# A warped-image transformer block on one core: 16 groups of 4 x 8 pixels, gathers in two bursts an image, one strips load moved

## The reference, cut to what matters

```python
x = x + rigid(x, dx, angle)   # each pixel: bilinear sample of its own image at a rotated, shifted place
x = x + ffn(x)                # relu(x wi^T + 2 x a^T b^T + expert lora) -> the same with wo; F = 2048
x = x + pooled(x)             # tanh scores, masked softmax over rows, p @ x / count
x = x + adapter(x)            # per-language 512 -> 128 -> 512, residual, layer norm, gamma, beta

# in rigid(X, dx, angle):
xp = c * gx - s * gy + dx[:, 0]
yp = s * gx + c * gy + dx[:, 1]
ix = (yp / h * 2.0 + 1.0) * 0.5 * (w - 1)
iy = (xp / w * 2.0 + 1.0) * 0.5 * (h - 1)
out = the four neighbours of (iy, ix), weighted by distance, 0 outside the image
```

## Time and profile before

| | |
|---|---|
| three runs | 2302.42, 2303.27, 2307.72 us (median 2303.27) |
| the profiled execution | 2311.27 us, span from first to last instruction 2309.6 |
| PE, DVE, ACT, POOL busy | 2098.2, 1964.2, 874.6, 947.5 us |
| granted TensorE clock, mean | 0.958 of full speed |
| gathers (L584) | 512, 1.32 us each on POOL |
| products (L853) | 4,096, 0.284 us each on DVE |

### The profile page before, as it was taken

The page is one execution under the profiler, slowest core; times in us unless marked ns, Lnnn a source line. Parts: engine busy times, 40 slices in busy tenths (PEclk is TensorE's granted clock), DMA queues, the critical chain, the costliest instruction groups (busy, mean ns, idle before and its releaser), DMA issues.

```text
span 2309.6 us, 53794 instructions
## 1 busy us (share of the span) xinstructions
PE 2098.2 (91%) x15230; PEld 1453.4 (63%) x15230; DVE 1964.2 (85%) x6594; ACT 874.6 (38%) x2292; POOL 947.5 (41%) x1066
## 2 busy tenths in 40 slices
PE   7678999989989998999999899999999989999996
PEld 3336667666666676666666666666666666667673
DVE  7578899989888898889989898898888898899943
ACT  2323444433433443343334343333433333344431
POOL 3434444454453444434434443453344344444201
PEclk9659999999999999999999999999999999999997
DMA  8683555665555556545655664465566455554322
GB/s 220 151 214 85 129 142 131 143 150 128 134 115 133 129 130 151 129 129 117 148 126 129 141 151 123 110 143 131 128 132 149 118 116 138 128 136 114 98 72 64
DMA packets 336489, 303.57 MB, mean 131 GB/s; under 512 B 187294, under 2 KB 255976, under 8 KB 335766
## 3 DMA queue, kind: packets, MB, share of 16 engines
q1 hardware_dynamic: 290358, 184.05, 33.1%
q0 software_dynamic: 42624, 109.35, 20.2%
q10 hardware_dynamic: 3168, 6.29, 0.9%
HBM read 273.73 MB, written 65.70 MB: 147 GB/s over the span
## 4 chain that ended last, share of the span: by engine, by line
DVE 46%; PE 28%; issue 15%; DVEq 5%; SPq 2%; DMA 1%; another core or an unknown queue 1%; ACT 1%; POOL 0%; ACTq 0%; POOLq 0%
DVE work L853 17%; PE bank L1343 9%; PE bank L1381 8%; DVE work L866 4%; DVE work L867 4%; DVE work L865 4%; DVEq L849 2%; DVEq L838 2%; DVE work L809 2%; PE bank L1199 2%; DVE warp_sum L880 2%; DVE hidden_parts L913 2%; PE bank L1375 1%; DVE warp_sum L876 1%; PE bank L1275 1%
## 5 line engine op out<-in xcount | busy, mean ns | idle before, releaser
L1343 PE MATMUL bank<-x1T,wiT 128*128 128x256 f16 x6144 | 765.3, 275 | 15.6 <-issue 14.8
L1381 PE MATMUL bank<-woT,hidden_parts 128*128 128x512 f16 x3072 | 755.9, 383 | 0.0
L853 DVE TENSOR_TENSOR work<-work 128x72 f32<-128x72 f32 x4096 | 683.5, 284 | 70.5 <-issue 48.2
L584 POOL DMA_INDIRECT work<-strips,gather_now x512 | 675.9, 1320 | 158.9 <-issue 136.6
L1343 PEld LDWEIGHTS bank<-x1T,wiT 128*128 128x128 f16 x6144 | 602.6, 99 | 163.7 <-issue 67.3
L1167 ACT ACTIVATE hidden<-bank 128x256 f32<-128x256 f32 x512 | 196.7, 384 | 767.0 <-PE bank L1350 446.8
L1381 PEld LDWEIGHTS bank<-woT,hidden_parts 128*128 128x128 f16 x3072 | 281.9, 99 | 247.2 <-issue 9.8
L580 POOL TENSOR_TENSOR gather_now<-group_now,no_offset 128x8 int32<-128x8 int32 x64 | 30.5, 476 | 792.9 <-DVE work L853 792.4
L913 DVE TENSOR_TENSOR hidden_parts<-hidden,hidden_parts 128x512 f16<-128x512 f32 x256 | 176.9, 691 | 29.2 <-ACT hidden_parts L1169 13.5
L1375 PE MATMUL bank<-hidden_parts,experts 128*128 128x128 f16 x2048 | 200.7, 221 | 0.0
L1169 ACT ACTIVATE hidden_parts<-bank 128x256 f16<-128x256 f32 x512 | 195.1, 381 | 0.0
(11 more groups left out here) (191 smaller groups left out, 2402.9 us busy)
## 6 DMA issues: line engine op xcount, KB each, us to landing
strips<-in_x_dram SPq DMA_DIRECT2D x64, 532.0 KB
lw<-in_L_cond_W_dram SPq DMA_DIRECT2D x128, 256.0 KB
xs<-in_x_dram SPq DMA_DIRECT2D x64, 256.0 KB
experts<-ib_dram SPq DMA_DIRECT2D x64, 256.0 KB
gamma_b<-in_L_cond_gamma_dram SPq DMA_DIRECT2D x64, 256.0 KB
x<-in_L_cond_beta_dram POOLq DMA_DIRECT2D x64, 256.0 KB, 5.9
out_dram<-y SPq DMA_DIRECT2D x64, 256.0 KB, 2.5
work<-strips,gather_now POOLq DMA_INDIRECT x512
```

The lines of the kernel that those rows point to most:

```text
L584: g.indirect_dma_start(out=win[:, k, gi, :], out_offset=None, in_=flat, in_offset=bass.IndirectOffsetOnAxis(at, 0)).then_inc(gathered[k], 16)
L853: last = v.tensor_tensor(prods[:, :, :, j, :, row].rearrange("p a b g -> p g b a"), seen, wx.unsqueeze(2).broadcast_to([128, NG, TAPS, TAP ...
L1343: t.matmul(b[:, 0:2 * T], wiT[:, ws, m, tile(f)], x1T[:, xs_, m, :], start=(m == 0 and ws + xs_ == 0), stop=False)
L1381: last = t.matmul(down_ps[k][:, :], hidden_parts[:, hs, f % RING, k * T:(k + 1) * T], woT[:, ws, f, :], start=(first and n == 0), stop=False)
```

## The change

- A group is 4 columns by 8 rows (`GC`, `GR`), and a partition holds 16 groups instead of 8. `Q` is 32 instead of 64, so an image takes 32 product instructions of 144 elements, 16 gathers of 226 elements, and 8 offsets a register load.
- The strips have 64 columns instead of 76, and an image takes three strip transfers instead of five.
- `gather` sends only the groups `first` to `end`. Each image's 16 gathers go in two bursts of eight. Image 0's second burst waits for `hidden_low(4)` of the pair, image 1's second burst for `hidden_low(0)` of the next pair and stands behind `add_beta` there.
- SP loads image 0's strips at the beginning of the pair instead of behind `load_lang`.
- The Newton iteration moves from POOL to DVE (`deviations`, 12 instructions with the guess, just ahead of `finish`); POOL does none of it.
- DVE's loop has four bodies a turn instead of two (`Fori(1, NP // 4 - 1)`).
- The address tables ahead of the loop have 1,024 columns instead of 512 and lie in `work`. `beta_b` is gone; its staging use goes to `x1T`.

```diff
-GP = 8
-NG = 8
-Q = GP * GP
+GC, GR = 4, 8
+NG = 16
+Q = GC * GR
 HALF = Q // 2
-LOADED = 32
...
-SW, SS = 76, 32
-LEFT = 2 * SS
+SW, SS = 64, 32
+LEFT = SS
...
-RUN = 4 * SW + 44
+RUN = 3 * SW + 34
...
-                src = bass.AP(img.tensor, img.offset, [[SS, NS - 5], [D, T], [1, SW]])
-                sp.dma_start(strips[s, 2:NS - 3, rows, :], src).then_inc(strips_in[s], 16)
-                for n in range(2):
-                    before = LEFT - n * SS
-                    sp.dma_start(strips[s, n, rows, before:SW], img[:, 0:SW - before]).then_inc(strips_in[s], 16)
-                    left = LEFT - n * SS
-                    sp.dma_start(strips[s, NS - 3 + n, rows, 0:left], img[:, D - left:D]).then_inc(strips_in[s], 16)
+                src = bass.AP(img.tensor, img.offset, [[SS, NS - 3], [D, T], [1, SW]])
+                sp.dma_start(strips[s, 1:NS - 2, rows, :], src).then_inc(strips_in[s], 16)
+                sp.dma_start(strips[s, 0, rows, LEFT:SW], img[:, 0:SW - LEFT]).then_inc(strips_in[s], 16)
+                sp.dma_start(strips[s, NS - 2, rows, 0:SS], img[:, D - SS:D]).then_inc(strips_in[s], 16)
...
             def body(i, q):
+                if there(i, -3):
+                    load_strips(i + 3, 0, 1 - q)
                 if there(i, 0):
                     load_expert_oa(i)
...
-            def gather(a, k, par):
+            def gather(a, k, par, first=0, end=NG, lows=None):
 
                 n, s = a * 2 + k, 2 * par + k
                 pool.sem_clear(pool_chain)
-                pool.wait_ge(pix_in[s], (a - par) * 24 + 48)
-                pool.wait_ge(strips_in[s], (a - par) * 40 + 80)
-                ge(pool, win_used, n - 1)
+                if not first:
+                    pool.wait_ge(pix_in[s], (a - par) * 24 + 48)
+                    pool.wait_ge(strips_in[s], (a - par) * 24 + 48)
+                    ge(pool, win_used, n - 1)
+                if lows is not None:
+                    pool.wait_ge(hidden_ready, lows)
...
             def body(i, q):
                 if there(i, 2):
                     add_beta(i - 2, q)
-                    deviations(i - 2)
-                for k in range(2):
-                    if there(i, -2):
-                        gather(i + 2, k, q)
+                if there(i, -1) and there(i, 0):
+                    gather(i + 1, 1, 1 - q, NG // 2, NG, i * (FT // 2) + 1)
+                if there(i, -2):
+                    gather(i + 2, 0, q, 0, NG // 2)
+                    gather(i + 2, 0, q, NG // 2, NG, i * (FT // 2) + 5 if there(i, 0) else None)
+                    gather(i + 2, 1, q, 0, NG // 2)
...
-                def guess_deviations():
+                def deviations():
 
                     link(v.tensor_scalar(var_eps[:, :], mv[:, :, 1], EPS, None, ALU.add))
                     link(v.tensor_scalar(guess_i[:, :], var_eps[:, :].bitcast(i32), 1, None, ALU.arith_shift_right))
-                    v.tensor_scalar(rstd[:, :].bitcast(i32), guess_i[:, :], -1.0, float(0x5F3759DF), ALU.mult, ALU.add).then_inc(guess_ready, 1)
+                    link(v.tensor_scalar(rstd[:, :].bitcast(i32), guess_i[:, :], -1.0, float(0x5F3759DF), ALU.mult, ALU.add))
+                    for step in range(3):
+                        link(v.tensor_tensor(newton[:, :], rstd[:, :], rstd[:, :], ALU.mult))
+                        link(v.scalar_tensor_tensor(newton[:, :], newton[:, :], -0.5, var_eps[:, :], ALU.mult, ALU.mult))
+                        link(v.scalar_tensor_tensor(rstd[:, :], newton[:, :], 1.5, rstd[:, :], ALU.add, ALU.mult))
...
-            with dve.Fori(2, NP // 2 - 1) as i:
-                body(i * 2 - 1, 1, first=False)
-                body(i * 2, 0)
-                body(i * 2 + 1, 1, second=False)
+            with dve.Fori(1, NP // 4 - 1) as i:
+                body(i * 4 - 1, 1, first=False)
+                for n in range(3):
+                    body(i * 4 + n, n % 2)
+                body(i * 4 + 3, 1, second=False)
```

More of the change, by code:

```diff
@@ L571, in _ @@
             flat = bass.AP(strips.tensor, 0, [[1, SLOTS * SLOT], [1, 1]])
-            def gather(a, k, par):
+            def gather(a, k, par, first=0, end=NG, lows=None):
                 n, s = a * 2 + k, 2 * par + k
                 pool.sem_clear(pool_chain)
-                pool.wait_ge(pix_in[s], (a - par) * 24 + 48)
-                pool.wait_ge(strips_in[s], (a - par) * 40 + 80)
-                ge(pool, win_used, n - 1)
+                if not first:
[4 more added lines that the diff above has]
+                    pool.wait_ge(hidden_ready, lows)
                 here = group_now[:, s, 2 * NG:NT].bitcast(i32)
-                g.tensor_tensor(gather_now[:, k, :], here, no_offset[:, :], ALU.add).then_inc(pool_chain, 1)
+                g.tensor_tensor(gather_now[:, k, first:end], here[:, first:end], no_offset[:, first:end], ALU.add).then_inc(pool_chain, 1)
                 pool.wait_ge(pool_chain, 1)
-                for gi in range(NG):
+                for gi in range(first, end):
                     at = gather_now[:, k, gi:gi + 1]
@@ L690, in _ @@
             first_column = stats[:, 0, 0:1]
-            link(v.tensor_scalar(first_column, part[:, 1:2], float(GP), None, ALU.mult))
+            link(v.tensor_scalar(first_column, part[:, 1:2], float(2 * GC), None, ALU.mult))
             link(v.tensor_scalar(group[:, 0, :], group[:, 0, :], first_column, None, ALU.add))
@@ L720, in floor @@
                 link(v.tensor_tensor(whole, whole, over, ALU.subtract))
-            xs_flat = xs[:, 1, :, :].rearrange("p k d -> p (k d)")
-            x1T_flat = x1T[:, :, :, :].rearrange("p s k t -> p (s k t)").bitcast(fp32)
             M = B * NG
             shape = lambda t: t.rearrange("p (b g) -> p b g", g=NG)
-            pos, other = xs_flat[:, 0:M], xs_flat[:, M:2 * M]
-            whole, whole_i = x1T_flat[:, 0:M], x1T_flat[:, M:2 * M].bitcast(i32)
-            at_f = y[:, 1, 0:M]
+            pos, other, whole, whole_i, at_f = (work[:, (n + 4) * M:(n + 5) * M] for n in range(5))
+            whole_i = whole_i.bitcast(i32)
             for ax in range(2):
@@ L845, in products @@
                     for m in range(start, end):
-                        j, row = m // GP, m % GP
+                        j, row = m // GR, m % GR
                         if m == 0:
@@ L981, in body @@
                             load_offsets(0, part)
-                        products(0, 0, 0, 16)
+                        products(0, 0, 0, 8)
                     if warp:
-                        products(0, 0, 16, 24)
+                        products(0, 0, 8, 12)
                     if ffn:
@@ L991, in body @@
                             residual(k)
-                    if there(i, 2):
-                        guess_deviations()
                     if warp:
-                        products(0, 0, 24, HALF)
+                        products(0, 0, 12, HALF)
                     hidden_low(0)
@@ L1002, in body @@
                     if there(i, 2):
+                        deviations()
                         finish(i - 2)
@@ L1008, in body @@
                 if warp:
-                    products(0, 1, 0, 8)
+                    products(0, 1, 0, 4)
                 hidden_low(2)
                 if warp:
-                    products(0, 1, 8, HALF)
+                    products(0, 1, 4, HALF)
                     take_offsets(1)
@@ L1029, in body @@
                 if warp:
-                    products(1, 1, 0, 24)
+                    products(1, 1, 0, 12)
                 hidden_low(6)
                 if warp:
-                    products(1, 1, 24, HALF)
+                    products(1, 1, 12, HALF)
                 if tail:
@@ L1050, in body @@
                 if ahead:
-                    products(0, 0, 0, 16, w + 1)
+                    products(0, 0, 0, 8, w + 1)
                 if ffn:
@@ L1057, in _ @@
             body(3, 1, second=False)
-            with dve.Fori(2, NP // 2 - 1) as i:
-                body(i * 2 - 1, 1, first=False)
-                body(i * 2, 0)
-                body(i * 2 + 1, 1, second=False)
-            body(NP - 3, 1, first=False)
-            for i in range(NP - 2, NP + 2):
+            with dve.Fori(1, NP // 4 - 1) as i:
[3 more added lines that the diff above has]
+                body(i * 4 + 3, 1, second=False)
+            body(NP - 5, 1, first=False)
+            for i in range(NP - 4, NP + 2):
                 body(i, i % 2)
```

72 lines of the change are left out of this document (27 added, 45 removed).

## The result

The changed kernel took 2603.63 us in the median (2587.33 to 2626.43, 4 runs), the kernel before 2305.49 in the runs beside it (2302.42 to 2317.82, 4 runs): ratio 1.1233, 95% interval 1.1185 to 1.128. It is 12% slower; I had forecast 2187 and 5% faster. The profiled execution, of 2626.43 us, was a slow one, 1.5% over the fastest, and is not in the ratio. A second profile, of 2623.69 us, reads alike: PE busy 84% of the span, DVE 74%, POOL 48%.

The account below looks back on a forecast made before the run. PE and DVE shared the limit, DVE ending plain pairs and PE's floor near 59.5 us. From 2309.6, -96 - 30 - 4 - 3 + 18 - 1.5 gives 2193.1, less 6.3 is 2187; range 2145 to 2245.

Parts of the forecast that it names:

- The nearest cover is 9 us, so I count nothing: Gathers in the loop: each burst lands at least 9 us before its products, so they add nothing to the pair.
- the gathers decide: Rival: at 15.8 us a burst POOL needs 67.6 a pair and image 1's products wait; 2349 us, chance 0.10.
- Products: DVE's products at L853: 64 of 144 elements, 0.232 us apart, replace 128 at 0.157; gain 5.3 us a pair.
- over 0.26: Sign of a wrong prediction: DVE's products start more than 0.26 us apart.
- Register loads: DVE's loads at L838 bring eight registers instead of 16; gain 1.2 us a pair, between 0 and 2.0.
- Newton iteration on DVE: Nine more chained DVE instructions cost 1.8 us a pair; POOL's 3.34 goes at the kernel's end, -1.5 overall there.
- Plain pair: A loop pair without branches falls from 63.5 to 60.2 us, limited by PE; 3.3 times 29 pairs gains 96.
- Branches: DVE's loop of four pairs takes five branches instead of twelve, each worth 4.26 us; gain 30 us.
- Cycle's end: Pairs that follow a cycle's end (65.25 us) lose half of their 1.7 surplus, 5 x 0.85 = 4 us gained.
- Prologue: Ahead of the loop, larger address tables and eight more gathers cost 18 us in all, bounds 8 and 30.
- The bursts' order: The loop's four gather bursts and their new waits hold only POOL's own queue; counted as nothing.
- The strips: Smaller strips, three transfers instead of five an image, image 0's earlier in SP's queue: nothing, or at worst a few us.

Follow-up runs that it names:

- set two: Runs on one chip: the changed kernel unchanged, 2614.21 us (ratio 1.1278), beside the kernel before, 2314.6, and variants of both.
- set three: Runs on another chip: the changed kernel unchanged, 2197.22 us (ratio 0.9577), beside the kernel before, 2293.6, and variants of both.
- set one: First follow-up runs, on one chip: single parts of the change and variants of its gathers, beside the kernel before, 2295.1 us.

## Why the prediction was wrong

**The step that failed** is "The nearest cover is 9 us, so I count nothing" of the gathers. I asked only whether a burst lands before its products, and they did land: DVE waits for no gather's landing in the loop. What I had no term for is that a dense row of gathers can hold up engines that don't touch its data: in the window of the result PE is busy 4.48 us of 13.6. On chips of the slow kind the changed kernel is 2614 against 2315 (set two) and on the other kind 2197 against 2294 (set three); +300 and -96, so the term is about 396 us on the first and about nothing on the second. It is shown that gathers are its cause on those chips (half of them gone: 2240; all of them, spaced wider: 2298). It is shown too that the waits (2778 without them), the order on DVE (it stands in half the gathers as it was) and the Newton iteration (2324 with it) are not. That it grows with the length of a dense row is shown by the table: 1.1 to 2.0 us for eight gathers, 4.27 for twelve, 5.0 to 7.3 for sixteen. My range knew of no such case: the rival "the gathers decide" had the right sign and the wrong mechanism, a window that comes late.

The trace of before hinted at it in one place, just behind the product row that I read in the earlier trace rows. At the end of its 16 gathers ahead of the loop (66.56 to 87.98), DVE's timeline goes on so:
```profile
86.49 0.29 DVE L853 TENSOR_TENSOR work<-work 128x72 f32<-128x72 f32 x1 [0.40 <-issue]
87.88 0.29 DVE L853 TENSOR_TENSOR work<-work 128x72 f32<-128x72 f32 x1 [1.10 <-issue]
88.58 0.28 DVE L853 TENSOR_TENSOR work<-work 128x72 f32<-128x72 f32 x1 [0.41 <-issue]
90.17 2.03 DVE L853 TENSOR_TENSOR work<-work 128x72 f32<-128x72 f32 x11 [1.31 <-issue]
```
Products that otherwise start 0.157 apart start 0.70, 1.39 or 1.59 apart and wait for nothing that the profile shows. In set one, with the same gathers on the other kind of chip, these 32 products ran in one piece of 5.11 us. So the chip of the trace that I predicted from was of the slow kind, and the symptom was in it. In the loop its rows of eight, with 9.5 us and more between them, have 0.2 us of gaps each. By its time the kernel before tells little: 2303 to 2320 us on the slow kind and 2293 to 2295 on the other.

Of the rival "the gathers decide" one reading was weak as well: it set the 1.70 us of a burst's first gather against 0.95, which is the eighth gather of the quiet row; the first one there took 1.07.

**The other terms**, on the chip where nothing covers them (forecast, then measured):
- Sum: 2303 - 2187 = 116 us; 2293.6 - 2197.2 = 96.4.
- Products: 0.232 from start to start and 0.36 long; twelve take 3.33 and one 0.43, so (3.33 - 0.43)/11 = 0.264. The gain a pair is 20.1 - 16.9 = 3.2 instead of 5.3. I had put "over 0.26" down as the mark of a wrong prediction; it did little harm, since PE was the limit by then. The contiguous 512-element row was not the right neighbour: 72 more elements cost 0.107 and not 0.075.
- Register loads: half as long (0.596 us for eight), and the idle time ahead of the fractions is 0.16 or nothing, where it was 0.36.
- Newton iteration on DVE: +1.8; the plain pair went from 63.7 (four-pair loop alone) to 65.5 (with it), which is just that, though on chips of different kinds; the whole run of set two says 1.3 a pair.
- Plain pair: 60.2; measured 60.7, with PE busy 60.0 and 60.3 and DVE 57.8.
- Branches: -30; measured -28.7.
- Cycle's end: I kept today's surplus (70.30 - 63.55 = 6.75). It is 9.7 now, in seven cycles about 20 us. The pair behind a cycle's end (63.50) is 2.8 over the plain one, where I had 0.85. The forecast's gain was too large by about the same 20 us on this chip, but only by luck: a plain pair is 0.5 longer than I said (some 14 us in 29), and the start of pair 0 is 14 us better than my 18, and these two cancel. Four windows of a cycle, as in the earlier trace rows:
```profile
720.90:781.60 60.70, 60.03 (x467) 42.95 (x465) 57.76 (x147) 26.60 (x70) 39.66 (x38) 1.00 0.58 153
781.60:842.40 60.80, 60.31 (x471) 43.41 (x469) 57.74 (x148) 26.60 (x70) 39.50 (x38) 1.00 0.60 156
842.40:912.80 70.40, 62.36 (x454) 43.83 (x452) 57.90 (x146) 26.11 (x69) 39.64 (x38) 0.93 0.55 142
912.80:976.30 63.50, 62.66 (x490) 45.33 (x488) 57.84 (x146) 26.90 (x71) 39.61 (x38) 0.99 0.51 142
```
 and PE's timeline in the third of these:
```profile
873.96 2.04 PE L1283 MATMUL bank<-x,probsT 128*128 128x512 f32 x2 [5.03 <-DVE x L920]
...
910.19 2.08 PE L1374 MATMUL bank<-x1T,experts 128*32 128x128 f16 x22 [3.01 <-issue]
```
 In a pair that PE ends, PE's own branch (3.01 ahead of L1374, 1.03 before) no longer lies in time that it would have waited for DVE, and DVE's (4.20) still makes add_pooled late by 5.03.
- Prologue: +18; first low_i at 166.5, against 162.2 with the old tiling on such a chip: +4.3. The first product came at 92.4 and not 103, so the address tables and eight more gathers cost 9 us and not 21. On the slow kind 181.8 and 183.3 look like my 181, and that is luck: the first product is at 92.2 there too, and most of the 17 us between the two kinds come from the window 100 to 116.
- The bursts' order: nothing, as forecast, on this kind of chip: half the gathers are not faster than all of them. Letting burst two go later costs 39 us; letting it go earlier was not tried. The strips were never changed alone, so their "nothing" is not tested.

**What stays open.** Why chips differ, and what is short: the profile names no releaser for the gaps, and the DMA engines are at 27% in them. That the supply of instructions is what is short is argued from the even 0.71 us and not shown. Whether it is the chip itself, or something about it that held for a set, is open too; one chip came up twice and was slow both times. Long rows in the loop of the kernel before's tiling (the doubled gathers) were never run on the slow kind; only its 16 gathers ahead of the loop show the same steps. No version here beats both kernels on both kinds: the changed one is best on the one (2197), half the gathers is no kernel, and the widely spaced one is 0.9% under before on the slow kind and was not run on the other.

## What to carry to other kernels

A queue of indirect DMAs that lands in time can still cost: before their number is doubled, look at how dense they lie (a gather takes 1.07 us for 904 bytes a partition and 1.32 for 1,392, so smaller ones save GpSimd little), and read "issue" and "remote" idle time of engines that don't use them. Run such a change on more than one chip: this one is 4% faster on one kind and 13% slower on another, while the kernel before differs by 1%.

## What the runs showed of the hardware that I had not expected

- On three of six chips, while GpSimd issues gathers 1.25 us apart, PE gets an instruction every 0.71 to 0.76 us, or none for several us, and ACT none for up to 9.4 us in the window shown. In the loop that begins at the seventh to ninth gather of a row and ends mostly 1 to 2.5 us after its last. Ahead of the loop DVE is held up in the same way, but only from the 23rd gather of a row of 32 on (26 instructions from 92.22 to 99.04 run undisturbed), until 4.7 us after its last. At 1.71 us apart the steps of 0.71 are gone (1 such start instead of 129) and a row of eight has 0.45 us of gaps instead of 1.14; on the other three chips there is nothing of it at 1.25 either.
- It costs more than the gaps: PE's matmuls also run slower. The granted clock was 0.67 in the starved window and 0.92 in the one after it, against 1.00 ahead of it; the levels in the trace are 1.00 and 0.50.
- The Trainium skill, Runtime: NRT & Kernel Launch, section on instruction fetch mechanics, says that each engine's sequencer streams its instructions over a DMA queue of its own in blocks of 16 KiB while it executes, mostly hidden. The traces agree that there are such queues, and the two rows below (packets, MB, share of the engines' time; packets of 16,384 bytes on q8, mostly 8,192 on q14) are those of the changed kernel at 2626.43 us and word for word those of its run in set three. Late blocks are not what spaces PE's instructions in the window shown: in the trace's DMA records no packet of either queue starts between 945.61 and 970.01 us, while PE goes on at 0.71 to 0.76 us and ACT comes back at 968.31. In other rows packets fall among the gaps. What else could hold up an engine's instructions no run here shows.
```profile
q8 instruction: 137, 2.24, 0.4%
q14 instruction: 161, 1.32, 0.2%
```
